# Stacks of queries and keys kept as fp32r and turned by products with an fp32r identity

## What is computed

```python
# attention A: causal softmax, with a layer norm of each head's q and k
q = _layernorm(q, gq, bq); k = _layernorm(k, gk, bk)
scores = where(causal, einsum('nhld,nhmd->nhlm', q, k), NEG)
out = einsum('nhlm,nhmd->nhld', softmax(scores), v)
# attention B: weights from distances, no softmax
sq = q2 + swapaxes(k2, -1, -2) - 2.0 * einsum('bhqd,bhkd->bhqk', Q, K)
W = (1e-4 + sqrt(maximum(sq, 0.0))) ** (-2)
W = W / (1e-4 + sum(W, axis=-1, keepdims=True))
O = G * einsum('bhqk,bhkd->bhqd', W, V)
```

## Time and profile before

| | us |
|---|---|
| median of 3 runs | 4340.56 (4340.33 to 4345.66) |
| the profiled execution, its own time | 4337.58 |
| its span, first to last instruction | 4335.3 |
| TensorE busy | 3583.2 (83%) |
| TensorE weight loads busy | 2580.9 (60%) |
| VectorE busy | 2565.9 (59%) |
| ScalarE busy | 2235.6 (52%) |
| GpSimd busy | 904.0 (21%) |
| mean granted TensorE clock | 0.897 |

### The profile page before, as it was taken

One profiled execution on the slowest core, in us unless ns is written; L12 is line 12 of the kernel. 1 busy time (PEld: TensorE's weight loads), 2 busy tenths in 40 slices (PEclk: granted clock), 3 DMA queues, 4 the chain that ended last, 5 costly groups with the idle time before them and its releaser, 6 DMA issues. The chain is left out here.

```text
span 4335.3 us, 55982 instructions
## 1 busy us (share of the span) xinstructions
PE 3583.2 (83%) x21924; PEld 2580.9 (60%) x21924; DVE 2565.9 (59%) x3967; ACT 2235.6 (52%) x2873; POOL 904.0 (21%) x882
## 2 busy tenths in 40 slices
PE   2788888897999999994667766766775899999998
PEld 2444444545888899993222332322321688889998
DVE  2556555553443345554988888898888544335554
ACT  1354545554332234442877878878888432224443
POOL 2222222210002201212332232132120001210112
PEclk9799999998999999996867777777777999999999
DMA  3000000001001013422000000000000100102432
GB/s 111 1 1 1 1 1 1 1 1 59 6 22 36 28 65 90 107 66 63 0 1 1 1 1 1 1 1 1 1 1 1 59 11 25 38 17 76 120 84 54
DMA packets 86807, 124.93 MB, mean 29 GB/s; under 512 B 7767, under 2 KB 73257, under 8 KB 86544
## 3 DMA queue, kind: packets, MB, share of 16 engines
q1 hardware_dynamic: 68880, 100.18, 6.8%
q0 software_dynamic: 17664, 21.17, 2.9%
HBM read 85.15 MB, written 42.55 MB: 29 GB/s over the span
## 5 line engine op out<-in xcount | busy, mean ns | idle before, releaser
L1827 DVE TENSOR_TENSOR b_w<-b_w 128x2048 f32<-128x2048 f32 x256 | 585.2, 2317 | 36.8 <-ACT b_w L1909 28.2
L472 DVE TENSOR_REDUCE a_mxp<-a_deep 128x1 f32<-128x512 f32 (+3 forms) x768 | 392.2, 552 | 355.3 <-PE a_deep L652 294.3
L1867 ACT ACTIVATE b_w<-b_ring 128x1024 f32<-128x1024 f32 x512 | 496.5, 1022 | 174.9 <-PE b_ring L1951 143.1
L1939 PE MATMUL b_acc<-b_w,b_vg 128*32 128x512 f32 x2048 | 331.0, 731 | 182.9 <-DVE b_w L1827 182.6
L1909 ACT ACTIVATE b_w<-b_w 128x2048 f32<-128x2048 f32 x256 | 468.0, 1897 | 1.4
L1381 ACT ACTIVATE f1hid<-f1ring 128x512 f32<-128x512 f32 (+2 forms) x256 | 132.6, 518 | 577.6 <-PE f1ring L1461 560.5
L1381 ACT ACTIVATE f2hid<-f2ring 128x512 f32<-128x512 f32 (+2 forms) x256 | 132.6, 518 | 576.6 <-PE f2ring L1461 559.6
L571 ACT ACTIVATE a_prob<-a_wide 128x1024 f32<-128x1024 f32 (+1 forms) x320 | 294.2, 943 | 239.2 <-PE a_wide L682 164.9
L1299 DVE TENSOR_TENSOR f1hid<-f1hid,f1ring 128x512 f32<-128x512 f32 (+2 forms) x256 | 150.2, 587 | 440.2 <-ACT f1hid L1381 440.1
L1299 DVE TENSOR_TENSOR f2hid<-f2hid,f2ring 128x512 f32<-128x512 f32 (+2 forms) x256 | 150.2, 587 | 438.6 <-ACT f2hid L1381 438.5
L1951 PE MATMUL b_ring<-b_qT,b_kT 64*128 64x512 f32 x1024 | 278.1, 573 | 142.0 <-ACT b_w L1867 121.2
(11 more groups left out here) (348 smaller groups left out, 6816.8 us busy)
## 6 DMA issues: line engine op xcount, KB each, us to landing
X<-expert_in SPq DMA_DIRECT2D x16, 650.0 KB, 4.8
expert_in<-zeros SPq DMA_DIRECT2D x8, 650.0 KB, 8.0
X<-in_x SPq DMA_DIRECT2D x4, 1024.0 KB, 9.6
x_mid<-X SPq DMA_DIRECT2D x8, 512.0 KB, 3.2
f1raw_x<-in_rd SPq DMA_DIRECT2D x4, 1024.0 KB, 5.3
f1raw_xf<-in_rg SPq DMA_DIRECT2D x4, 1024.0 KB, 5.1
f1raw_xf<-in_ru SPq DMA_DIRECT2D x4, 1024.0 KB, 7.2
f1raw_g<-in_rg SPq DMA_DIRECT2D x4, 1024.0 KB, 4.9
```

Of the source, the lines that this page charges most:

```text
L472: v.tensor_reduce(mxp[:, t, 2 * e + h, i:i + 1], dslot(step, h)[:, 0:n], AX_X, ALU.max).then_inc(s_dve, 1)
L1827: v.tensor_tensor(one(m), one(m), one(m), ALU.mult).then_inc(s_wts, 1)
L1867: s.activation(w[:, m, 2 * pair:2 * pair + 2, :].rearrange("p h n -> p (h n)"), slot(at + pair), ACT.Ln, scale=SHEP_EPS ** -2).then_inc(R. ...
L1939: last = pe.matmul(acc[32 * h:32 * h + 32, qc, :], vg[:, u % 2, h, x, :], w[:, x, h, :], start=(x == 0), stop=(x == TB - 1))
```

## The change

In both attentions `qs` and `ks` become fp32r tiles, and a new fp32r tile `identr` [128, 128] takes a copy of the identity, made by GpSimd before `s_init`. The copies that wrote fp32r through a `bitcast` now write the tile as it is; memsets and reads go through a `bitcast` to fp32. The subtraction that makes the low part now writes fp32r. The three places where TensorE turns a stack (lines 636, 660, 1984) issue an ordinary product with `identr` in place of `transpose` with `ident`. Order, semaphores, slots, and all other transposes (tokens, turn, back, FFN) stay.

```diff
-        qs = sb("qs", [P, 2, TB, HG * KC])
-        ks = sb("ks", [P, TB, HG * KC])
+        qs = sb("qs", [P, 2, TB, HG * KC], F32R)
+        ks = sb("ks", [P, TB, HG * KC], F32R)
+        identr = sb("identr", [P, P], F32R)
...
-            eng.tensor_copy(st[:, :, 0:DH].bitcast(F32R), one)
-            eng.tensor_copy(st[:, :, hi2:hi2 + DH].bitcast(F32R), one)
+            eng.tensor_copy(st[:, :, 0:DH], one)
+            eng.tensor_copy(st[:, :, hi2:hi2 + DH], one)
             if side == 0 and u > 1:
-                eng.memset(st[:, :, 3 * DH:3 * DH + 2], 0.0)
+                eng.memset(st[:, :, 3 * DH:3 * DH + 2].bitcast(F32), 0.0)
             eng.drain()
-            return eng.tensor_tensor(st[:, :, lo:lo + DH], one, st[:, :, 0:DH], ALU.subtract)
+            return eng.tensor_tensor(st[:, :, lo:lo + DH], one, st[:, :, 0:DH].bitcast(F32), ALU.subtract)
...
-                pool.memset(qs[:], 0.0)
-                pool.memset(ks[:], 0.0)
+                pool.memset(qs[:].bitcast(F32), 0.0)
+                pool.memset(ks[:].bitcast(F32), 0.0)
+                pool.tensor_copy(identr[:], c["ident"][:])
...
                         for t in range(TB):
-                            last = pe.transpose(dst[:, t * P:(t + 1) * P], src[:, t, e * P:(e + 1) * P], ident[:])
+                            last = pe.matmul(dst[:, t * P:(t + 1) * P], src[:, t, e * P:(e + 1) * P], identr[:], start=True, stop=True)
...
                         for t in range(TB):
-                            last = pe.transpose(dst[:, t * P:(t + 1) * P], qs[:, u % 2, t, e * P:(e + 1) * P], ident[:])
+                            last = pe.matmul(dst[:, t * P:(t + 1) * P], qs[:, u % 2, t, e * P:(e + 1) * P], identr[:],
+                                             start=True, stop=True)
...
                         for t in range(TB):
-                            last = pe.transpose(slot(n)[:, t * P:(t + 1) * P], (ks if STACKS[x][1] else qs)[:, t, :], ident[:])
+                            last = pe.matmul(slot(n)[:, t * P:(t + 1) * P], (ks if STACKS[x][1] else qs)[:, t, :], identr[:],
+                                             start=True, stop=True)
```

More of the change, by code:

```diff
@@ L372, in _ @@
                 kv = ks[:].rearrange("p t (h n) -> p (t h) n", n=KC)
-                pool.memset(kv[:, :, 3 * DH:3 * DH + 2], 1.0)
+                pool.memset(kv[:, :, 3 * DH:3 * DH + 2].bitcast(F32), 1.0)
                 for i in range(3):
@@ L483, in _ @@
                         dve.drain()
-                        v.tensor_scalar(st[:, :, :, 3 * DH].bitcast(F32R), mine, -1.0, None, ALU.mult)
+                        v.tensor_scalar(st[:, :, :, 3 * DH], mine, -1.0, None, ALU.mult)
                         dve.drain()
-                        v.tensor_tensor(rest, st[:, :, :, 3 * DH], mine, ALU.add)
+                        v.tensor_tensor(rest, st[:, :, :, 3 * DH].bitcast(F32), mine, ALU.add)
                         dve.drain()
-                        v.tensor_scalar(st[:, :, :, 3 * DH + 1].bitcast(F32R), rest, -1.0, None, ALU.mult).then_inc(s_neg, 1)
+                        v.tensor_scalar(st[:, :, :, 3 * DH + 1], rest, -1.0, None, ALU.mult).then_inc(s_neg, 1)
                     elif what == "back":
@@ L1567, in attention_b @@
         gated = sb("gated", [P, TB, D])
-        qs = sb("qs", [P, TB, 2 * KC])
-        ks = sb("ks", [P, TB, 2 * KC])
+        qs = sb("qs", [P, TB, 2 * KC], F32R)
+        ks = sb("ks", [P, TB, 2 * KC], F32R)
+        identr = sb("identr", [P, P], F32R)
         vg = sb("vg", [P, 2, HG, TB, 32])
@@ L1662, in build @@
                         pool.wait_ge(s_qkT, len(STACKS) * n + i - 1)
-                    pool.tensor_copy(st[:, :, :, 0:DH].bitcast(F32R), src)
-                    pool.tensor_copy(st[:, :, :, hi2:hi2 + DH].bitcast(F32R), src)
-                    pool.tensor_copy(st[:, :, :, at:at + 1].bitcast(F32R), norm)
+                    pool.tensor_copy(st[:, :, :, 0:DH], src)
+                    pool.tensor_copy(st[:, :, :, hi2:hi2 + DH], src)
+                    pool.tensor_copy(st[:, :, :, at:at + 1], norm)
                     pool.drain()
-                    pool.tensor_tensor(st[:, :, :, lo:lo + DH], src, st[:, :, :, 0:DH], ALU.subtract)
-                    pool.tensor_tensor(st[:, :, :, at + 1:at + 2], norm, st[:, :, :, at:at + 1], ALU.subtract)
+                    pool.tensor_tensor(st[:, :, :, lo:lo + DH], src, st[:, :, :, 0:DH].bitcast(F32), ALU.subtract)
+                    pool.tensor_tensor(st[:, :, :, at + 1:at + 2], norm, st[:, :, :, at:at + 1].bitcast(F32), ALU.subtract)
                     pool.drain().then_inc(s_stack, 1)
                 pool.memset(vg[:], 0.0)
-                pool.memset(qs[:], 0.0)
-                pool.memset(ks[:], 0.0)
+                pool.memset(qs[:].bitcast(F32), 0.0)
+                pool.memset(ks[:].bitcast(F32), 0.0)
+                pool.tensor_copy(identr[:], c["ident"][:])
                 pool.drain()
                 for h in range(2):
-                    pool.memset(qs[:, :, h * KC + 3 * DH + 2:h * KC + 3 * DH + 4], 1.0)
-                    pool.memset(ks[:, :, h * KC + 3 * DH:h * KC + 3 * DH + 2], 1.0)
+                    pool.memset(qs[:, :, h * KC + 3 * DH + 2:h * KC + 3 * DH + 4].bitcast(F32), 1.0)
+                    pool.memset(ks[:, :, h * KC + 3 * DH:h * KC + 3 * DH + 2].bitcast(F32), 1.0)
                 pool.memset(vg[:, :, :, :, DH:DH + 1], 1.0)
```

## The result

The changed kernel is slower: 4395.24 us (4390.98 to 4401.61) against 4340.44 us before, ratio 1.0127, 95% interval 1.0109 to 1.0144. The forecast had the side right (+26 us), and its size was less than half of the +55 us. The profiled execution took 4401.6 us, 64 us over that of before.

What follows compares the result with a forecast made beforehand. TensorE and its clock were taken to bound attention A, but seldom B. Terms 3.1 + 18 + 6 + 0.3 summed to +27 us on the profiled 4337.58 us, 4365; forecast 4366 us, range 4339 to 4389.

Steps and rivals of the forecast that it cites:

- What bounds: TensorE ends last in attention A and its clock sets its speed; in B it mostly follows ScalarE and VectorE.
- The trains, +3.1 us: Rows of stack products in A: 120 ns a tile against 116, +4 ns x 768 tiles; B's 512 hidden.
- The product's length: Each 128-column fp32r stack product takes 219 ns, 54 ns shorter than the fp32 transpose's 273.
- one more pass of the transpose: The old transpose's 273 ns against 219 meant one more 54 ns pass of its columns through the array.
- The clock of A, +18 us: Less array work in A's stack turns makes the granted clock fall more often or rise later, +18 us.
- 12 x 1.5: In A, dips or late rises in about 8 of 16 units plus 4 more, each 1.5 us: +18 us.
- My upper bound: For A's clock: one dip in each unit and six late rises, 22 x 1.5 = +33 us.
- The clock of B, +6 us: In B the stretch before ScalarE's restart stays at half clock, 15 x 0.4 = +6 us, bounds 0 and +22.
- GpSimd 0 and start +0.3 us: GpSimd's fp32r subtraction costs nothing more; copying the identity before A's first unit costs +0.3 us.
- The indifferent clock: Rival: the clock does not care, only +3.4 us stay, 4341 to 4344 us; chance 0.20.
- The faster rival: Rival: transposes hardly feed the clock and ordinary products do, lifting it in A and B, 4322 us; chance 0.10.
- The range: Whole kernel's time, 8 in 10: 4339 to 4389 us, from indifferent clock to upper bounds taken in part.

Runs made afterwards that it cites:

- wide256: Changed kernel with products in attention A alone, six of eight widened to 256 columns, the excess overwritten; B by fp32 transposes: 4354.5 us, 1.0023 of the kernel before.
- neg_wide: Changed kernel with products only in A's second turning of the queries (neg), 256 columns in six of eight; all else fp32 transposes: 4341.3 us, ratio 0.9998.
- neg_only: Changed kernel with 128-column products only in both neg steps of A (256 of 768 tiles); all other stacks by fp32 transposes: 4396.1 us, ratio 1.0122.
- late: Changed kernel with all stacks by fp32 transposes, plus sixteen useless 8-column products delaying the second neg step of each unit of A: 4395.7 us, ratio 1.0127.
- neg_fill: Changed kernel with products only in A's neg steps, and output-row turning in each unit's second score step done three times: 4369.0 us, ratio 1.0064.
- neg_second: Changed kernel with products only in the second neg step of each unit of A (128 of 768 tiles); all else fp32 transposes: 4364.7 us, ratio 1.0046.
- b_only: Changed kernel with products in attention B alone; A's stacks turned by fp32 transposes as before: 4337.6 us, ratio 0.9996.
- types_only: Changed kernel keeping fp32r tiles, identity copy and fp32r subtractions, but turning all stacks by fp32 transposes: 4340.2 us, ratio 0.9992.
- stack_only: Changed kernel with products only in A's stack steps (512 of 768 tiles); neg steps and B by fp32 transposes: 4375.6 us, ratio 1.0076.
- the added work: Changed kernel in full, with output-row turning in the second score step of each unit of A done three times: 4393.9 us, ratio 1.0113.
- neg_first: Changed kernel with products only in the first neg step of each unit of A; all else by fp32 transposes: 4337.3 us, ratio 0.9989.

## Why the prediction was wrong, step by step

- **What bounds.** Right: TensorE in A, not in B.
- **The trains, +3.1 us.** The units at full clock show no loss (55.2 and 55.2 us). The load was right at 192 ns, and 119 ns a tile against the 120 taken. The product's length, from the slope between 256 and 512 columns and from line 648, was wrong (276 for 219 ns): below 256 columns the recorded length did not go on falling. (The 388 ns that I took for 512 columns is, in the earlier trace rows, the longest product of a line of 256 columns.) With it goes the reading of 273 against 219 ns as one more pass of the transpose. That the transposes put more through the array than one pass of 128 columns follows from the clock behind them, not from their length.
- **The clock of A, +18 us. This is the term that was mis-sized: 64 us.** The mechanism, fewer columns through the array and so a lower clock in A, was right and is shown by wide256 and neg_wide. The price of time at half clock was right too: 1.5 us for 3.1 us is 0.48, measured 0.41. What failed is the number of dips and their length: "12 x 1.5". I counted 12 dips of 3.1 us, 37 us at half clock, and took them as independent of one another. The runs show 157 us more instead, and most of them in long spells: A has six of over 20 us, 167 us together, where before there was one of 34. In neg_only such a spell stands behind a dip: the dip delays the unit, the clock falls again behind a thin stretch further on, and it stays down for 27 us. That the delay is what makes the stretch thin, and that the transposes of the first neg had ended such spells, is argued from the traces and from late and neg_fill, and not shown by itself. In the full kernel the late rises weigh too: they are the rises on transposes of which I had counted four, at 1.5 us each. The two that open a batch, behind 446 and 685 us, each come after 24 us at half clock in place of 10. My upper bound, one in each unit and six late rises, 33 us, excluded this: it bounded the number of first dips and not how long one lasts. neg_second (+20 us), where long spells are rare, comes near to my 18 us.
- **The clock of B, +6 us.** The clock fell as said (0.76 to 0.72 or 0.73), and cost nothing (b_only 0.9996). That the last value group stands at half clock where ScalarE restarts doesn't count, as ScalarE's wait shows (140.7 us for 143.1 in the earlier trace rows). The step failed in pricing half-clock units of B by 41.8 against 41.1 us: the two do the same steps (132 and 133 instructions of TensorE), what makes the 0.7 us isn't shown, and by b_only a lower clock doesn't lengthen B.
- **GpSimd 0 and start +0.3 us.** Right, by types_only, line 1671 and the 279 ns copy.
- **Rivals.** The indifferent clock (0.20) is refuted by the falling clock in both attentions. The faster rival (0.10) is refuted too: ordinary products in place of transposes lowered the clock of A from 0.92 to 0.85. The Trainium skill, page "TensorE: Matmul & The Clock Gate", section "Part 4: PE-mode transpose", has it that transpose-mode does not count as activity for the clock gate. These traces contradict that for fp32 transposes.
- **The range** ended at 4389, six us short. A term that can feed back on itself should have had its upper end from long spells, of which the trace of before has one of 34 us, and not from a count of dips.

What stays open: in the full kernel three of the six long spells begin before 170 us and two in units that open a batch, and the added work didn't touch these five. They come with the stack steps (stack_only has them too, neg_only doesn't); how they and neg_only's chains add up to the whole wasn't separated. Why neg_first is a little faster isn't settled: its trace has 24 us less at half clock than before, but is of the fastest of its ten runs, 10 us under their median.

## What to carry to other kernels

On TensorE, an instruction that does less in the array can cost more than it saves, though it takes no longer itself: check what it does to the granted clock there and in the stretches that follow, and not its own time alone. Before replacing an operation, look for places where the clock rises behind it; they show what depends on it. When a dip delays an engine that others pace, price it by the spell that can follow, from the longest spell in the trace, and test with useless columns, which change the array's work and, up to 256 columns here, the trains by 0.04 us in eight.

## What the runs showed of the hardware

- The clock rises behind a run of fp32 transposes, and behind fp32r products of the same 128 columns it rises later: at 88.3 us before and at 97.7 after. With fp32r products of 256 columns the clock of A is nearly that of the transposes (0.91 for 0.92, and 0.92 in neg_wide).
- A busy TensorE is not enough for full clock: in neg_only it was busy for 25.5 of 27.1 us, with products of 64 rows, and stayed at 0.50.
- An fp32r product of 128 columns in a train is recorded with 276 ns; at the end of a PSUM bank in wide256, behind products of 256 columns, with 234 to 238 ns on average over all clocks (317 to 339 for 256 columns). Its recorded length depends on what stands around it:

```profile
L640 PE MATMUL a_wide<-a_identr,a_ks 128*128 128x256 f32 x192 | 36.6, 319 | 0.0
...
L640 PE MATMUL a_wide<-a_identr,a_ks 128*128 128x128 f32 x64 | 15.0, 234 | 0.0
```

- GpSimd writes an fp32r result of a subtraction at the price of an fp32 one (1032 and 1033 ns for 128x256).
